# The spectral stage of a pre-norm decoder layer: products grouped by array tiling, other PSUM banks, and another order on five engines

## What is computed

```python
def _autocorrelation(Q, K, V):                   # K = V = ctx, 8 heads of 64
    qf, kf = fft(q, axis=2), fft(k, axis=2)
    corr = ifft(qf * conj(kf), axis=2).real
    w, idx = top_k(corr.transpose(0, 1, 3, 2), 8)    # 8 lags for each channel
    w = softmax(w, axis=-1)
    for i in range(8):
        g = minimum(idx[..., i] + pos, L - 1)
        out = out + w[..., i] * take_along_axis(v, g, axis=2)
...
logits = einsum('bsd,ed->bse', x, route_w)
topk_v, topk_idx = top_k(logits, 1)
route_weight = one_hot(topk_idx[..., 0], 8) * topk_v
h = einsum('bsd,erd->bser', x, A)
out = einsum('bser,eor->bso', route_weight[..., None] * h, Bw)
...
x = x + dense(layernorm(x))
x = x + autocorrelation(layernorm(x), ctx, ctx)
x = x + experts(layernorm(x))
```

## Time and profile before

| what | us |
|---|---|
| median of 3 runs | 821.62 (819.18 to 824.54) |
| profiled execution | 823.87 |
| its span | 821.8 |
| PE busy | 764.2 (93%) |
| DVE busy | 577.7 (70%) |
| ACT busy | 409.6 (50%) |
| POOL busy | 264.1 (32%) |

### The profile page before, as it was taken

How to read it: one execution, slowest core, us unless ns; L and a number is a source line. 1 busy time by engine, 2 the same in 40 slices (tenths; PEclk the granted TensorE clock), 3 DMA queues, 4 the chain that set the end, 5 groups by cost and what they waited for, 6 DMA issues and landing times.

```text
span 821.8 us, 10558 instructions
## 1 busy us (share of the span) xinstructions
PE 764.2 (93%) x3384; PEld 550.2 (67%) x3384; DVE 577.7 (70%) x1291; ACT 409.6 (50%) x743; POOL 264.1 (32%) x196
## 2 busy tenths in 40 slices
PE   3879999999999999999999999999997889999975
PEld 1335778778888888888888888887774445455432
DVE  4998874667897386566657737642457999999983
ACT  7794753564755355255354445521223646566531
POOL 0001121023453342433333333321211445444451
PEclk9999999999999999999999999999999989999997
DMA  8464210012322022113103201120252535665301
GB/s 209 141 235 141 73 51 1 1 39 74 106 79 103 19 84 81 35 39 104 63 15 100 78 26 52 38 72 1 64 128 65 130 95 136 154 155 140 79 26 38
DMA packets 31285, 67.26 MB, mean 82 GB/s; under 512 B 4800, under 2 KB 5184, under 8 KB 31232
## 3 DMA queue, kind: packets, MB, share of 16 engines
q1 hardware_dynamic: 31232, 66.60, 28.1%
HBM read 45.61 MB, written 4.19 MB: 61 GB/s over the span
## 4 chain that ended last, share of the span: by engine, by line
PE 66%; DVE 22%; issue 5%; ACT 3%; POOL 2%; DMA 1%; SPq 0%; DVEq 0%; POOLq 0%; ACTq 0%
PE ps L666 19%; PE ps L668 19%; PE ps L667 19%; DVE mark L1001 2%; DVE pp L959 2%; DVE top L983 2%; POOL pn L1097 1%; DVE wl L1042 1%; PE ps L637 1%; DVE stats L535 1%; DVE st L837 1%; PE ps L882 1%; DMA lb<-in_lora_attn_b 1%; DVE pc L1088 1%; PE ps L1113 1%
## 5 line engine op out<-in xcount | busy, mean ns | idle before, releaser
L666 PE MATMUL ps<-x_hi,w_hi 128*128 128x512 f32 x448 | 176.2, 393 | 0.2 <-POOL w_lo L523 0.2
L668 PE MATMUL ps<-x_hi,w_lo 128*128 128x512 f32 x448 | 174.7, 390 | 0.0
L667 PE MATMUL ps<-x_lo,w_hi 128*128 128x512 f32 x448 | 174.4, 389 | 0.0
L782 POOL TENSOR_TENSOR h_lo<-hf,h_hi 128x512 fp32r<-128x512 f32 x56 | 73.9, 1320 | 244.6 <-ACT h_hi L777 244.5
L791 DVE TENSOR_TENSOR acc<-acc,ps 128x512 f32<-128x512 f32 x112 | 76.4, 685 | 73.4 <-PE ps L668 73.4
L770 DVE TENSOR_TENSOR hf<-hf,ps 128x512 f32<-128x512 f32 x56 | 38.4, 686 | 86.9 <-PE ps L668 86.9
L523 POOL TENSOR_TENSOR w_lo<-wt,w_hi 128x512 fp32r<-128x512 f32 x42 | 62.3, 1484 | 113.9 <-ACT w_hi L516 113.9
L666 PEld LDWEIGHTS ps<-x_hi,w_hi 128*128 128x128 f32 x448 | 84.1, 188 | 21.7 <-issue 4.0
L668 PEld LDWEIGHTS ps<-x_hi,w_lo 128*128 128x128 f32 x448 | 84.1, 188 | 17.9
L667 PEld LDWEIGHTS ps<-x_lo,w_hi 128*128 128x128 f32 x448 | 84.2, 188 | 17.3
L666 PE MATMUL ps<-w_hi,h_hi 128*128 128x512 f32 x224 | 87.9, 393 | 1.9 <-DVE acc L717 1.4
(11 more groups left out here) (150 smaller groups left out, 1352.2 us busy)
## 6 DMA issues: line engine op xcount, KB each, us to landing
codes_sb<-in_codes SPq DMA_DIRECT2D x40, 256.0 KB, 3.0
scale_sb<-in_scale_rows SPq DMA_DIRECT2D x80, 128.0 KB, 2.9
kc<-ku SPq DMA_DIRECT2D x64, 128.0 KB, 2.4
kx<-ku SPq DMA_DIRECT2D x32, 256.0 KB, 3.8
lft<-in_lora_ft SPq DMA_DIRECT2D x14, 512.0 KB, 4.4
acc<-in_x SPq DMA_DIRECT2D x4, 1024.0 KB, 8.4
ctx<-in_ctx SPq DMA_DIRECT2D x16, 256.0 KB, 3.8
out<-fin SPq DMA_DIRECT2D x16, 256.0 KB, 3.8
```

Of the source, the lines that this page charges most:

```text
L666: nc.tensor.matmul(bank, hi, rhs_hi, start=start, stop=False)
L667: nc.tensor.matmul(bank, hi, rhs_lo, start=False, stop=False)
L668: return nc.tensor.matmul(bank, lo, rhs_hi, start=False, stop=stop)
L782: nc.gpsimd.tensor_tensor(h_lo[:, c % 2, i], hf[:, i], h_hi[:, c % 2, i].bitcast(F32), ALU.subtract).then_inc(hlo_done, 1)
```

## The change

- VectorE's same (L1097 after) reads the weights' transform from its PSUM banks `KW` in place of the copy `wu`; ScalarE still copies `wu`, for cross alone.
- The context's transform from tile 3 on goes to the query's banks `QW`, the expert's product and final to `GATHER`. One list per bank group (`wide`, `query`, `misc`, `inverse`) says who used it last; `wait_for_last` waits for its reader.
- Chains on VectorE are cut into single steps and laid between others: the five routing steps, sum and reciprocal, the statistics of the third norm; top and mark are cut in halves of four rows. Stats and mean are now at the end of the slot before that of variance and Newton.
- All five lists have a new order and new offsets. GpSimd's is cross, divide, power in place of cross, power, divide, for the same tiles.
- TensorE's list puts weights and context together (both with 64 rows of input), then the products with 128 rows. SyncE's spread and context load stand a slot earlier.

The diff, cut to its core:

```diff
...
+    def dve_square(dve, t, b):
+        dve.wait_ge(pow3, t + 1)
+        nc.vector.tensor_tensor(na3[:, b], pw3[:, b], pw3[:, b], ALU.mult).then_inc(scaled3, 1)
+
+    def dve_residual(dve, t, b):
+        dve.wait_ge(scaled3, 4 * t + 1)
+        nc.vector.scalar_tensor_tensor(out=nb3[:, b], in0=na3[:, b], scalar=-0.5, in1=ve3[:, b],
+                                       op0=ALU.mult, op1=ALU.mult).then_inc(scaled3, 1)
+
...
-        n = 4 * t
-        dve.wait_ge(pow3, t + 1)
-        newton(dve, scaled3, n, ve3[:, b], pw3[:, b], na3[:, b], nb3[:, b], rs3[:, b])
-        dve.wait_ge(scaled3, n + 3)
+        dve.wait_ge(scaled3, 4 * t + 2)
+        nc.vector.scalar_tensor_tensor(out=rs3[:, b], in0=nb3[:, b], scalar=1.5, in1=pw3[:, b],
+                                       op0=ALU.add, op1=ALU.mult).then_inc(scaled3, 1)
+
...
+    FORWARD, BACKWARD, QUERY, LAGS, TURN_H, EXPERT, GATHERED = range(7)
+    emptied = (ku_copied, psame, prod, lag_copied, h_copied, fin_done, x3_done)
+    wide = [(FORWARD, 0), (FORWARD, 1), (FORWARD, 2), (QUERY, 0)]
+    for v in range(TT + 3):
+        wide += [(BACKWARD, v - 1)] * (0 <= v - 1 < TT)
+    query = []
+    for v in range(TT + 3):
+        query += [(QUERY, v + 1)] * (1 <= v + 1 < TT) + [(FORWARD, v + 3)] * (3 <= v + 3 < TT)
+    misc = [(LAGS, 0)]
+    for v in range(TT + 3):
+        misc += [(LAGS, v - 1)] * (1 <= v - 1 < TT) + [(TURN_H, v - 2)] * (0 <= v - 2 < TT)
+    inverse = []
+    for v in range(TT + 3):
+        inverse += [(GATHERED, v - 2)] * (0 <= v - 2 < TT) + [(EXPERT, v - 3)] * (0 <= v - 3 < TT)
...
-        wait_for_wide(pe, FORWARD, t)
-        by_sequence(pe, KW, KU, ctx[:, b]).then_inc(ku_ready, 1)
+        wait_for_last(pe, query if t > 2 else wide, FORWARD, t)
+        by_sequence(pe, QW if t > 2 else KW, KU, ctx[:, b]).then_inc(ku_ready, 1)
...
-        if real(t - 1):
-            act.wait_ge(psame, t - 1)
+        if real(2 * (t - 1)):
             act.wait_ge(pcross, 2 * (t - 1))
         nc.scalar.copy(wu[:, b], pair(KW)).then_inc(w_copied, 1)
...
-        nc.vector.tensor_tensor(pc[:, b], wu[:, b], ku[:, t % KU_RING], ALU.mult).then_inc(psame, 1)
+        nc.vector.tensor_tensor(pc[:, b], pair(KW), ku[:, t % KU_RING], ALU.mult).then_inc(psame, 1)
...
-            if t == 0:
-                pass
-            else:
-                pe.wait_ge(x3_done, t)
+            wait_for_last(pe, inverse, GATHERED, t)
...
-        wait_for_misc(pe, EXPERT, t)
-        nc.tensor.matmul(ps[:, MISC], wht[:, b], eb[:], start=True, stop=True).then_inc(expert, 1)
+        wait_for_last(pe, inverse, EXPERT, t)
+        nc.tensor.matmul(ps[:, GATHER], wht[:, b], eb[:], start=True, stop=True).then_inc(expert, 1)
...
-        nc.vector.tensor_tensor(fin[:, b], x3[:, b], ps[:, MISC], ALU.add).then_inc(fin_done, 1)
+        nc.vector.tensor_tensor(fin[:, b], x3[:, b], ps[:, GATHER], ALU.add).then_inc(fin_done, 1)
...
-                if a := at(-2, 3):
+                if a := at(-3, 3):
                     sp_spread(sp, *a[:2])
-                if a := at(-4, 5):
+                if a := at(-5, 5):
                     sp_ctx(sp, *a[:2])
...
                     x_pow(pool, NCH + 2 + a[0] // 4)
-                if a := at(2):
+                if a := at(1):
                     pool_cross(pool, *a[:2])
-                if a := at(2):
+                if a := at(-1, 1):
+                    pool_divide(pool, *a[:2])
+                if a := at(1):
                     pool_pow(pool, *a[:2])
-                if a := at(0, 1):
-                    pool_divide(pool, *a[:2])
-            slots(pool, piece, 2)
+            slots(pool, piece, 1)
 
...
             def piece(at):
+                if a := at(4):
+                    act_turn_h(act, *a[:2])
+                if a := at(1, 1):
+                    act_exp_top(act, *a[:2])
                 if a := at(2, 1):
                     act_lags(act, *a[:2])
+                if a := at(1, 1):
+                    act_exp(act, *a[:2])
+                if a := at(2):
+                    act_w(act, *a[:2])
+                if a := at(-2, 3):
+                    act_ku(act, a[0])
                 if a := at(4):
                     act_expert(act, *a[:2])
-                if a := at(1, 1):
-                    act_exp(act, *a[:2])
-                if a := at(1, 1):
-                    act_exp_top(act, *a[:2])
-                if a := at(2):
-                    act_w(act, *a[:2])
+                if a := at(-2, 2):
+                    act_normalise_x2(act, *a[:2])
                 if a := at(3):
                     act_normalise_x3(act, *a[:2])
-                if a := at(3):
-                    act_turn_h(act, *a[:2])
-                if a := at(-2, 3):
-                    act_ku(act, a[0])
-                if a := at(-2, 2):
-                    act_normalise_x2(act, *a[:2])
             slots(act, piece, 4)
...
             def piece(at):
                 if a := at(3):
-                    dve_x3(dve, *a[:2])
+                    dve_variance(dve, *a[:2])
                 if a := at(1, 1):
-                    dve_top_less(dve, *a[:2])
+                    dve_weigh(dve, *a[:2])
                 if a := at(3):
-                    dve_stats(dve, *a[:2])
-                if a := at(0, 1):
-                    dve_product(dve, *a[:2])
+                    dve_square(dve, *a[:2])
+                if a := at(3):
+                    dve_residual(dve, *a[:2])
                 if a := at(3):
                     dve_rstd(dve, *a[:2])
+                if a := at(3):
+                    dve_shift(dve, *a[:2])
                 if (a := at(2)) and a[0] in LATER:
                     x_rstd(dve, NCH + 2 + a[0] // 4)
                 if (a := at(0)) and a[0] in LATER:
                     x_stats(dve, NCH + 2 + a[0] // 4)
-                if a := at(1, 1):
-                    dve_sum(dve, *a[:2])
-                if a := at(4):
-                    dve_final(dve, *a)
                 if a := at(2):
                     dve_same(dve, *a[:2])
                 if a := at(0, 1):
-                    dve_top(dve, *a[:2])
-                if a := at(1, 1):
-                    dve_weigh(dve, *a[:2])
+                    dve_top(dve, *a[:2], 0)
                 if a := at(0, 1):
-                    dve_mark(dve, *a[:2])
+                    dve_top(dve, *a[:2], 1)
+                if a := at(4):
+                    dve_final(dve, *a)
+                if a := at(0, 1):
+                    dve_mark(dve, *a[:2], 0)
+                if a := at(0, 1):
+                    dve_less(dve, *a[:2])
+                if a := at(0, 1):
+                    dve_negate(dve, *a[:2])
+                if a := at(0, 1):
+                    dve_mark(dve, *a[:2], 1)
                 if a := at(3):
-                    dve_route(dve, *a[:2])
+                    dve_best(dve, *a[:2])
+                if a := at(0, 1):
+                    dve_sum(dve, *a[:2])
+                if a := at(3):
+                    dve_ties(dve, *a[:2])
+                if a := at(-1, 1):
+                    dve_product(dve, *a[:2])
+                if a := at(3):
+                    dve_first(dve, *a[:2])
+                if a := at(0, 1):
+                    dve_invert(dve, *a[:2])
+                if a := at(3):
+                    dve_chosen(dve, *a[:2])
+                if a := at(2):
+                    dve_x3(dve, *a[:2])
+                if a := at(3):
+                    dve_hidden(dve, *a[:2])
+                if a := at(2):
+                    dve_stats(dve, *a[:2])
+                if a := at(2):
+                    dve_mean(dve, *a[:2])
             slots(dve, piece, 4)
...
             def piece(at):
-                if a := at(0, 2):
+                if a := at(-1, 2):
                     pe_q(pe, *a[:2])
-                if a := at(2):
-                    pe_w(pe, *a[:2])
-                if a := at(4):
-                    pe_expert(pe, *a[:2])
-                if a := at(0, 1):
-                    pe_corr(pe, *a[:2])
-                if a := at(3):
-                    pe_turn_h(pe, *a[:2])
-                if a := at(-2, 3):
-                    pe_ku(pe, *a)
+                if a := at(1, 1):
+                    pe_lags(pe, *a[:2])
                 if a := at(3):
                     pe_route(pe, *a[:2])
                 if a := at(2):
                     pe_gather(pe, *a[:2], 0)
                 if a := at(2):
                     pe_gather(pe, *a[:2], 1)
-                if a := at(1, 1):
-                    pe_lags(pe, *a[:2])
+                if a := at(1):
+                    pe_w(pe, *a[:2])
+                if a := at(-3, 3):
+                    pe_ku(pe, *a)
                 if a := at(3):
                     pe_turn_wh(pe, *a[:2])
-            slots(pe, piece, 4)
+                if a := at(-1, 1):
+                    pe_corr(pe, *a[:2])
+                if a := at(3):
+                    pe_expert(pe, *a[:2])
```

(50 more changed lines are left out.)

69 lines of the change are left out of this document (31 added, 38 removed).

## The result

The changed kernel took 860.08 us (median of 4 runs, 857.36 to 866.86) against 820.4 for the kernel before: 1.047 times as long, with a 95% interval of 1.0437 to 1.05. The direction was forecast, the size was not: 842 was expected, with 852 as the upper end of its range for 8 in 10. The profiled execution took 859.37, with a span of 857.2 against 821.8, so 35.4 us are to be explained.

What follows compares the result with a forecast made beforehand. VectorE's list, 10.70 us a steady tile, was taken as the bound; gains bring it to 9.6, the hold adds 2.55, making 12.1. Over all stretches +20.4 us moves the median from 821.62 to 842, 8-in-10 range 821 to 852.

Steps and rivals of the forecast that it cites:

- What bounds the kernel: Steady spectral tiles: VectorE's list of work is the period, 10.70 us, with no idle time; TensorE is close behind.
- The price of the hold: VectorE's Newton steps, next to GpSimd's cross: waiting for the shared SBUF port costs 2.55 us a tile, list 12.1.
- Both steps held: Main case, chance 0.70: cross's two halves each block a Newton step, square and residual over 1 us each; 834 to 851.
- rivals without a hold: Newton steps do not meet cross, which starts after them; TensorE bounds at 9.9 us a tile; 809 us, chance 0.15.
- one step held: Square starts ahead of cross, so only the residual is blocked; list 11.1 us a tile; 827 us, chance 0.10.
- third rival: Loop from gather through Newton steps and routing back, 12.0 us, gains half a microsecond more; 848 us and up, chance 0.05.
- the paragraph on the other engines: Spectral stage: TensorE's list of about 9.9 us, ScalarE and SP changes all hidden under VectorE's 12.1, at no cost.
- The gain of same: VectorE's same, reading PSUM in place of the SBUF copy, falls from 1.70 to 1.14 us: 0.56 a tile.
- The sum: Spectral stage by stretch: +3.0 to the fourth top, +2.4 next four tiles, +11.2 eight steady tiles, +3.8 drain: +20.4 us.

Runs made afterwards that it cites:

- the filled kernel: Changed kernel plus four unused products a tile on TensorE, where it waits for the normalised tile: 843.45 us, 1.027 times the time before.
- PSUM alone: Kernel before the change, with only same reading the weights' transform from PSUM in place of the SBUF copy: 825.01 us, 1.0033 times the time before.

## Why the prediction was right in direction and wrong in size

- **What bounds the kernel**, VectorE's list of 10.70 with TensorE close behind: nothing here speaks against it.
- **The price of the hold**: right, in place, size and share. Both steps held, 1.22 and 1.19; the list 12.11 to 12.13 where it sets the period, for 12.1. From the start of variance to the start of same it is 3.99 us in the filled kernel (743.76 to 747.75), where the forecast had worked out 4.00. The hold to which it gave 0.70 came, and the rivals without a hold or with one step held did not; but the time lies outside the 834 to 851 of that case, in the region of its third rival (848 and up), to which it gave 0.05.
- **The failing step** is the paragraph on the other engines. It put TensorE's list without its waits at about 9.9 (9.92 measured at clock 1.00) and had all of it "hidden under VectorE, at nothing". A list of 9.9 under a period of 12.1 leaves TensorE over 2 us of wait a tile, and the forecast never asked what the clock does behind such a wait, though the earlier trace rows had it at 0.81 in the drain, where TensorE was busy for 25.48 of 39.19 us. At the lower clock the routing came 1.16 to 1.22 late. That is 1.34 a tile over six of the eight tiles, 8 us, and 7.5 more in the other stretches (3.7 in the four tiles ahead, 3.5 in the drain, the rest at the start): together the 15.5 that the fill gave back.
- **The third rival**, a loop that outruns the list, had the right shape at the wrong size: 12.0 was given for the loop at full clock, with half a microsecond more as the case to fear, and what would make it longer was not named. At the lower clock it was 13.44. The forecast had both halves in hand, the loop just under the list and a TensorE with idle time, and did not put them together.
- **The gain of same** (0.56): from same to top it is 1.14 as forecast, so the size stands in the sum, but it was credited to PSUM. The order gave it: from SBUF it was 1.22 as well, and PSUM alone lost 0.24 a tile in the order of before.
- **The sum** without the clock was +20.4 and is +19.9. That it is this close owes something to luck: the drain was 1.3 short in it (+5.1 for +3.8), and the stretches up to the eighth top were 2.1 too long together.

## What to carry to other kernels

Where a slower engine is forecast to hide another one, work out how long the hidden one will stand idle in each period, and if that is TensorE, whether the work right behind its wait is on a chain that closes on the slow engine: work that is hidden at the full clock need not stay hidden at half of it. A small instruction of VectorE with two SBUF inputs is best written with a column scalar when GpSimd may be at work beside it (0.21 us for 1.22 here). And a gain measured in one order (an instruction that sheds a hold) belongs to that order: look at what it had been holding off.

## What was not expected of the hardware

- More work made the program faster: four useless products a tile took 857.2 us of span to 841.7.
- The same wait of TensorE at the same place left the clock at its upper level in some runs and was followed by the lower one in others: the first wait for product (2.01 us) in two kernels that differ only in where same reads, the second (2.46) in two runs of one kernel. That is probably what spread one kernel's runs over two groups 8 us apart. In the changed kernel a wait of 2.78 left it up, and the next, of 2.19, did not. Which it will be was not settled. The Trainium skill (TensorE: Matmul & The Clock Gate, "HAM oscillation — how this bites in real kernels") describes a kernel in which TensorE waits for a transfer in every pass of its loop and starts every pass at the lower clock; the tiles of 13.44 us behave like it (0.87 to 0.88 in each) with a wait for other engines in place of a transfer, and the two of 12.1 (1.00) do not.
